# Five sums of squares per tile in two single-pass products instead of one 32-bit product

## The reference

```
x = layernorm(x + delta_rule_attention(x))     # ln1, and a norm over each head inside
x = layernorm(x + top-2-of-8 experts(x))       # ln2
x = layernorm(x + gated_linear_scan(x))        # ln3
x = layernorm(x + gated FFN of 3 stages(x))    # ln4

layernorm(x) = (x - mean(x)) / sqrt(var(x) + 1e-5)
inside the attention, for each head:
o = o * rsqrt(mean(o * o) + 1e-5) * norm_w
```

## Time and profile before

| | |
|---|---|
| median of 3 runs | 814.32 us (811.01 to 815.33) |
| the profiled execution | 817.33 us, of which the span shown is 815.3 us |
| PE busy | 752.2 us, 92% of the span |
| VectorE, ScalarE, GpSimd busy | 576.4, 499.7, 489.4 us |
| mean granted TensorE clock | 0.967 |
| the chain that ended last | PE 66%, DVE 11%, POOL 10%, ACT 5% |

### The profile page before, as it was taken

How to read it: one execution, slowest core, us unless ns; L and a number is a source line. 1 busy time by engine, 2 the same in 40 slices (tenths; PEclk the granted TensorE clock), 3 DMA queues, 4 the chain that set the end, 5 groups by cost and what they waited for, 6 DMA issues and landing times.

```text
span 815.3 us, 11346 instructions
## 1 busy us (share of the span) xinstructions
PE 752.2 (92%) x3492; PEld 579.7 (71%) x3492; DVE 576.4 (71%) x1146; ACT 499.7 (61%) x799; POOL 489.4 (60%) x503
## 2 busy tenths in 40 slices
PE   4999689888959999999989999999999999999996
PEld 3778567576547777767777778777876786777775
DVE  4677866779569757786768678867777777776553
ACT  3778444554755585468536855675577457767763
POOL 0049768579957766787675356534754475286353
PEclk9999896989979999999989999999999999999999
DMA  4025340652322320132012301400130120021000
GB/s 142 14 86 177 88 143 15 193 156 67 90 55 76 97 60 28 41 75 66 28 39 85 84 27 45 110 27 27 55 99 26 31 60 26 1 78 40 1 14 13
DMA packets 47244, 52.68 MB, mean 65 GB/s; under 512 B 2720, under 2 KB 31904, under 8 KB 47200
## 3 DMA queue, kind: packets, MB, share of 16 engines
q1 hardware_dynamic: 47200, 52.13, 22.0%
HBM read 38.62 MB, written 13.50 MB: 64 GB/s over the span
## 4 chain that ended last, share of the span: by engine, by line
PE 66%; DVE 11%; POOL 10%; ACT 5%; issue 5%; DMA 3%; SPq 0%; DVEq 0%; ACTq 0%; POOLq 0%
PE bank L461 66%; POOL fbl L1330 3%; POOL acc L1338 3%; POOL tmp L1270 1%; POOL tpm L1273 1%; DVE m L1632 1%; DMA pack<-pk 1%; POOL texp L1297 1%; DMA xs<-in_xh 1%; DVE sexp L1585 1%; DVE x L1568 1%; DVE spread L1577 1%; DVE yg L1595 1%; DVE x3h L1790 1%; DVE pk L1423 1%
## 5 line engine op out<-in xcount | busy, mean ns | idle before, releaser
L1330 POOL TENSOR_TENSOR fbl<-hf,fbh 128x512 fp32r<-128x512 f32 x64 | 90.0, 1406 | 44.1 <-ACT fbh L1127 43.5
L1270 POOL TENSOR_TENSOR tmp<-apm,tpm 128x31 f32<-128x31 f32 (+15 forms) x124 | 74.7, 603 | 55.4 <-DVE apm L1455 41.8
L1115 ACT ACTIVATE hf<-bank 128x512 f32<-128x512 f32 x64 | 38.3, 598 | 112.8 <-PE bank L461 97.7
L1773 DVE TENSOR_TENSOR fbl<-hf,fbh 128x512 fp32r<-128x512 f32 x64 | 68.9, 1077 | 48.4 <-ACT fbh L1121 48.4
L1273 POOL TENSOR_TENSOR tpm<-tpm,tmp 128x31 f32<-128x31 f32 (+15 forms) x124 | 76.6, 617 | 9.7
L1369 POOL TENSOR_TENSOR fbl<-hf,fbh 128x512 fp32r<-128x512 f32 x28 | 37.0, 1324 | 72.5 <-DVE fbh L1826 72.5
L1338 POOL TENSOR_TENSOR acc<-acc,yg 128x512 f32<-128x512 f32 x48 | 67.8, 1413 | 17.9 <-DVE yg L1595 17.9
L461 PE MATMUL bank<-fal,wfh 128*128 128x512 f32 x160 | 67.8, 424 | 0.0
L461 PE MATMUL bank<-fbl,wmh 128*128 128x512 f32 x128 | 58.8, 459 | 7.1 <-POOL fbl L1330 4.0
L461 PE MATMUL bank<-fah,wfh 128*128 128x512 f32 x160 | 62.5, 391 | 0.0
L461 PE MATMUL bank<-fah,wfl 128*128 128x512 f32 x160 | 62.3, 390 | 0.0
(11 more groups left out here) (238 smaller groups left out, 2146.3 us busy)
## 6 DMA issues: line engine op xcount, KB each, us to landing
gb<-gt SPq DMA_DIRECT2D x64, 256.0 KB, 3.2
pk<-pack SPq DMA_DIRECT2D x7, 1280.0 KB, 7.4
pack<-pk SPq DMA_DIRECT2D x5, 1280.0 KB, 7.1
ws<-in_wf SPq DMA_DIRECT2D x11, 256.0 KB, 3.6
pack<-pk SPq DMA_DIRECT2D x4, 640.0 KB, 4.4
xs<-in_xh SPq DMA_DIRECT2D x8, 262.0 KB, 2.8
xt<-in_xh SPq DMA_DIRECT2D x8, 262.0 KB, 3.0
ws<-in_wm SPq DMA_DIRECT2D x8, 256.0 KB, 3.7
```

What stands on the lines that cost most here:

```text
L1115: A.activation(hf[:, 0, :], bank[4][:, :], ACT.Gelu).then_inc(S["gelu_done"], 1)
L1270: G.tensor_tensor(m, a, r, ALU.mult).then_inc(S["t_mul"], 1)
L1330: G.tensor_tensor(fbl[:, sl, :], hf[:, 1, :], f32(fbh[:, sh, :]), ALU.subtract)\
L1773: tt(fbl[:, sl, :], hf[:, 0, :], f32(fbh[:, sh, :]), ALU.subtract).then_inc(S["lo0"], 1)
```

## The change

For 39 of the sums (eight each of the head sums and of ln1, ln2 and ln3, seven of ln4), ScalarE squares the tile twice: first with the output rounded to `F32R` (tiles `a5r`, `m4r`), then in full (`a2`, `m2`, `f2`), as before. VectorE subtracts the rounded squares from the full ones (`square_low`, `head_low`) into another rounded tile, the rest, which lies over the full squares (`a2r`, `m2r`, `f2r`). TensorE multiplies both, one single-pass product each, by a rounded copy of the constant matrix (`mean_r`, `head_r`), and adds them in the bank. It waits for the rounded squares before the first and for the rest before the second. Two copies at the program's start make `mean_r` and `head_r`. No tile takes new memory but `mean_r`.

The order changes in three places of a tail. `head_sums` moves on TensorE from behind `glu(1)` to behind `glu(2)`, and `var_product("2")` from behind `glu(2)` to behind `glu(3)`. On VectorE the subtractions are put between other work.

```diff
@@ tensor
             def var_product(n, t, src, bk):
-                pe.wait_ge(S["sq" + n], t + 1)
-                mm(bank[bk][:, :], mean_w, src[:, :]).then_inc(S["var" + n], 1)
+                pe.wait_ge(S["sq" + n], 2 * t + 1)
+                mm(bank[bk][:, :], mean_r[:, :], SQ_HIGH[n][:, :], stop=False)
+                pe.wait_ge(S[f"sq{n}_lo"], t + 1)
+                mm(bank[bk][:, :], mean_r[:, :], SQ_LOW[n][:, :], start=False).then_inc(S["var" + n], 1)
@@ head_sums
-                pe.wait_ge(S["osq_done"], a + 1)
+                pe.wait_ge(S["osq_done"], 2 * a + 1)
                 pe.wait_ge(*after("o_copied", CN * a + CN))
-                mm(bank[2][:, :], head_w, a2[:, :]).then_inc(S["oss_done"], 1)
+                mm(bank[2][:, :], head_r[:, :], a5r[:, :], stop=False)
+                pe.wait_ge(S["osq_lo"], a + 1)
+                mm(bank[2][:, :], head_r[:, :], a2r[:, :], start=False).then_inc(S["oss_done"], 1)
@@ tails on TensorE
                     glu(f, 1)
+                    glu(f, 2)
                 if a is not None:
                     head_sums(a)
                 if f is not None:
-                    glu(f, 2)
+                    glu(f, 3)
                 if m is not None:
                     var_product("2", m, m2, 1)
                 if f is not None:
-                    glu(f, 3)
                     pe.wait_ge(*after("g_act", FC * f + FC - 1))
@@ scalar (the same in head_squares and attention_square, with a5r)
                 act.wait_ge(*after("d" + n, t + 1))
+                A.activation(SQ_HIGH[n][:, :], src[:, :], ACT.Square).then_inc(S["sq" + n], 1)
                 A.activation(dst[:, :], src[:, :], ACT.Square).then_inc(S["sq" + n], 1)
@@ vector
+            def square_low(n, t, buf):
+                dve.wait_ge(S["sq" + n], 2 * t + 2)
+                tt(SQ_LOW[n][:, :], buf[:, :], f32(SQ_HIGH[n][:, :]), ALU.subtract).then_inc(S[f"sq{n}_lo"], 1)
+
+            def head_low(a):
+                dve.wait_ge(S["osq_done"], 2 * a + 2)
+                tt(a2r[:, :], a2[:, :], f32(a5r[:, :]), ALU.subtract).then_inc(S["osq_lo"], 1)
@@ ramp2 on VectorE (ramp3 alike)
+                head_low(a)
                 ...
                 unit_rows(s)
                 beta_rows(s)
+                square_low("1", a, a2)
                 attention_norm(a)
@@ dense on VectorE, behind gated(m, 3)
+                    if f is not None and e == 4:
+                        square_low("4", f, f2)
@@ tails on VectorE
                     glu(0)
+                    head_low(a)
                     glu(1)
+                    square_low("2", m, m2)
                     glu(2)
                     glu(3)
                 ...
-                    lru_input(m)
+                    lru_gx(m)
+                    square_low("1", a, a2)
+                    lru_m(m)
                 ...
                     attention_low(a)
+                    square_low("3", m, m2)
                     top_two(a)
@@ drain on VectorE, behind the cast of product 1
+                    if c == 1:
+                        square_low("4", l, f2)
```

More of the change, by code:

```diff
@@ L82, in build @@
         centre_w = sb("centre_w", [128, 128])
+        mean_r = sb("mean_r", [128, 128], F32R)
+        at_s3 = top[0]
         s3row = sb("s3row", [128, 128]); wsum = sb("wsum", [128, 24])
@@ L99, in build @@
         gb = sb("gb", [128, 2, W]); yg = sb("yg", [128, 2, W]); hf = sb("hf", [128, 2, W])
+        at_a = top[0]
         a1, a2, a3, a4, a5, oT = (sb(n, [128, W]) for n in ("a1", "a2", "a3", "a4", "a5", "oT"))
@@ L128, in build @@
         assert top[0] <= nc.sbuf_usable_end, top[0]
+        head_r = over("head_r", [128, 128], F32R, at_s3)
         wqkv = over("wqkv", [128, 3, 128], F32, temps)
@@ L196, in build @@
             texp_ready turn_done turn_ready in_done x_f x_ready os_done s_ready o_copied
+            osq_lo sq1_lo sq2_lo sq3_lo sq4_lo
             mixl_done mix_act mix_o o_ready osq_done oss_done ors_done og_done wo_done x1_hi
@@ L238, in f32 @@
             return ap.bitcast(F32)
+        a2r, a5r = (over(n, [128, W], F32R, at_a + 2048 * i) for n, i in (("a2r", 1), ("a5r", 4)))
+        m2r, m4r = (over(n, [128, W], F32R, temps + 2048 * i) for n, i in (("m2r", 1), ("m4r", 3)))
+        f2r = over("f2r", [128, W], F32R, at_f + 2048)
+        SQ_HIGH = {"1": a5r, "2": m4r, "3": m4r, "4": m4r}
+        SQ_LOW = {"1": a2r, "2": m2r, "3": m2r, "4": f2r}
         def by_seq(ap):
@@ L892, in drain @@
                     c = slice(g * W // 2, (g + 1) * W // 2)
-                    pe.wait_ge(S["sq4"], f + 1 + g)
+                    pe.wait_ge(S["sq4"], 2 * f + 1 + g)
                     mm(bank[3 - 3 * g][:, 0:W // 2], mean_w, f2[:, c]).then_inc(S["var4"], 1)
@@ L997, in head_squares @@
                 act.wait_ge(*after("o_ready", a + 1))
+                A.activation(a5r[:, :], a1[:, :], ACT.Square).then_inc(S["osq_done"], 1)
                 A.activation(a2[:, :], a1[:, :], ACT.Square).then_inc(S["osq_done"], 1)
@@ L1009, in attention_square @@
                 act.wait_ge(S["wo_done"], a + 1)
+                A.activation(a5r[:, :], bank[3][:, :], ACT.Square).then_inc(S["sq1"], 1)
                 A.activation(a2[:, :], bank[3][:, :], ACT.Square).then_inc(S["sq1"], 1)
@@ L1530, in _ @@
             tt(centre_w[:, :], ident, mean_w, ALU.subtract).then_inc(S["cen_ready"], 1)
+            V.tensor_copy(mean_r[:, :], mean_w)
             V.memset(sexp[:, :, :, :], 0.0)
@@ L1550, in _ @@
                     solve_out(0)
+                    V.tensor_copy(head_r[:, :], head_w)
                     V.memset(spread[:, 0:B, :, :], 0.0).then_inc(S["x_zero"], 1)
@@ L1837, in tails @@
                     glu(0)
+                if A_:
+                    head_low(a)
+                if F_:
                     glu(1)
+                if M_:
+                    square_low("2", m, m2)
+                if F_:
                     glu(2)
```

## The result

The changed kernel takes 823.47 us (median of 4 runs, 820.09 to 825.01) where the kernel before took 814.83 us beside it (4 runs, 811.01 to 817.67). The ratio is 1.0095, with a 95% interval of 1.0066 to 1.0124: it is slower, by 5 to 10 us. The forecast was 820.3 us.

What follows compares the result with a forecast made beforehand. TensorE was taken as the bound, tied with a second chain in every tail; 3.5 + 0 - 0.7 + 0 + 0.6 + 1.2 + 1.4 = 6.0 us on 814.32 gave 820.3 us, range 809 to 827.

Steps and rivals of the forecast that it cites:

- a second chain: Every tail: lru gates, tanh, ln1 square, table load, decay, scan, cast, GpSimd rest, hidden; claimed to tie with TensorE.
- step 4: Router at a steady tail's end: gate 1.8 later, TensorE 0.9 late; last GELU slips; next dense stage 0.7 late.
- TensorE's credit: TensorE saves 0.36 us a sum, 14.0 us over 39; rival that it arrives, in part or all, 0.14.
- Step 1: Steady tail, head and ln2 sums: credit 0.72, but the third gate product comes late; 0.2 us remains.
- Step 2: Steady tail, tied chain: extra ln1 square moves the table load +0.5; 0.2 earlier start leaves TensorE +0.3 us.
- Step 3: Steady tail, ln3's sum: the subtraction stands behind GpSimd's texp; TensorE is 0.5 us late.
- Dense stages: ln4 sums: wait for VectorE's bank about 0.6 instead of 0.20, no loss; two stages with triangular systems +0.3 each.
- signs named beforehand: Waits expected at gate product, GpSimd rest, gate_turn, yg and drain; table load 0.3 later; ln3 subtraction over 1.4 us.
- f = 5, f = 6, drain: Tail without t_spread: 0; tail without attention: -0.7; drain, ln4's sum waiting for its subtraction until 782.7: +1.2 us.
- The ramps: Second and third ramp: ln1's subtraction and extra squares delay chains, +0.7 us each, +1.4 together.
- the rival on the clock: Steady tails drop to 1.2 GHz: little chance; one more slow stretch gives 823; router or clock above 823: 0.16.

Runs made afterwards that it cites:

- e1: Changed kernel with only ln3's sum put back to one 32-bit product (no second square, no subtraction); 818.4 us.
- e3: Changed kernel with head sums and ln2's sum back to 32-bit products at their old place on TensorE; 822.3 us.
- e6: Changed kernel with the rest left out of all five sums: one rounded square, no subtraction, one single pass; 805.4 us.
- e8: Changed kernel with only ln4's sum put back to one 32-bit product; 820.0 us.
- e7: Changed kernel with two passes for head and ln3 alone, ln1, ln2, ln4 back, x1l behind the router's selection; 815.46 us, ratio 0.9986 to the kernel before.
- e2: Changed kernel with only ln1's sum put back to one 32-bit product; 822.6 us.
- e4: Changed kernel with ln3's subtraction moved ahead of x1l on VectorE; 827.6 us.
- e5: Changed kernel with ln3's subtraction ahead of the router's selection and x1l behind it; 822.4 us.
- e9: e7 with the router's gate weights moved right behind top_two, ahead of two casts and x1l; 816.75 us.
- e10: e5 with the same early gate weights, all five sums in two passes; 829.1 us.
- e11: e9 with the GELU table loaded ahead of the wait for GpSimd's rest and x1l behind the third cast; 814.63 us, ratio 0.998 to the kernel before.

## Why the prediction was right

The direction, its reason (TensorE ties with a second chain in every tail, and the change loads that chain) and the place (five tails, drain) held; e1 to e3, e6 and e8 show it part by part. That the size of a tail came out too is partly luck: steps 1 to 3 cost 0.78 where 0.5 was put down, and step 4, which was to lift that to 0.7 at the next stage, added nothing.

- **TensorE's credit.** 0.36 a sum was about right: 12.3 us less busy, and e7's tail of f = 5 shortens by 0.78 with two sums, 0.39 each.
- **Step 1**, forecast to keep 0.2, kept nothing. The third gate product was late and `hidden` began 0.27 earlier, as worked out. What I left out is the last chunk of `hidden`, which waits for GpSimd's last `fal` rest, 1.79 us long (608.54 in GpSimd's timeline). The first ln1 square moved by 0.03. e3 agrees: undoing this step leaves the period at 78.32.
- **Step 2**, forecast +0.3: +0.52, the second ln1 square in full, because step 1 had nothing to set against it. e2 gives back 0.45.
- **Step 3**, forecast +0.5 in all: the product behind the sum starts 0.78 late, of which 0.26 is this step's own, where I had 0.2. The wait (0.37) and the length (1.77) are those foreseen.
- **Step 4** failed. It had TensorE wait for `gate`, 0.9 late there and 0.7 in the next stage. The gate slipped by 1.72 (forecast 1.8), but TensorE, 0.28 later than forecast behind ln3's sum, came just with it: the products behind the sum are 0.78 late, `gate_turn` is 0.75 late, and no wait is marked between them. The last GELU, second in the step, lost the 0.90 of idle time that ScalarE had ahead of it, and no more: it still starts 0.03 behind TensorE's last product. So three chains now end the tail together, TensorE's own, the gate's and ScalarE's, and the first alone accounts for the 0.75. e1, which frees the other two and gives back 0.20, shows it. The tie is what e4, e5, e7, e9 and e10 each ran into. Of the signs named beforehand the wait for `gate` at `gate_turn` is the one that didn't come; the others did, the late table load with 0.52 in the place of 0.3.
- **Dense stages.** 0.60 of waiting in the place of 0.20, and nothing lost in the steady ones, as forecast. Between tails 0 and 1 it was +0.37 where 0.3 was put down. The +0.44 of the last dense stage I did not foresee: I had given a cost only to stages with triangular systems, and this one has none. e8 ties both to ln4. The stage between tails 1 and 2, also put at 0.3, costs about 0.9 at one clock (estimate above).
- **f = 5, f = 6, drain.** +0.2, -0.8 and +1.2 against 0, -0.7 and +1.2. The drain begins 1.15 us later in this trace. ScalarE's, VectorE's and TensorE's rows of it:

```profile
781.31 0.63 ACT L996 ACTIVATE m4r<-f 128x512 fp32r<-128x512 f32 x1 [2.08 <-DVE f L1946]
781.85 0.62 ACT L997 ACTIVATE f<-f 128x512 f32<-128x512 f32 x1
```

```profile
782.30 0.95 DVE L1941 CAST fah<-hf 128x512 fp32r<-128x512 f32 x1
783.17 0.68 DVE L1629 TENSOR_TENSOR f2r<-f,m4r 128x512 fp32r<-128x512 f32 x1
```

```profile
781.99 0.50 PE L472 MATMUL bank<-m4r,mean_r 128*128 128x512 f32 x1
783.90 0.50 PE L472 MATMUL bank<-f2r,mean_r 128*128 128x512 f32 x1 [1.41 <-DVE f2r L1629]
```

  The subtraction ends at 783.85 - 1.15 = 782.70, the very time put down, but on another way: it is held by the gate product and the cast ahead of it on VectorE, and meets no rest itself (0.68). Against the earlier trace rows, where TensorE ran on from 780.84 without a gap, it now waits 1.41 inside the sum.
- **The ramps**, +1.4, can't be judged: that stretch moves by 4 us between the profiled executions.
- **The clock.** The steady tails kept their 1.00, as the rival on the clock had it. But a stretch at a lower clock stood in the trace before and not in the one after, worth about 3.5 us, and it hides part of the loss when the two spans are compared.

The stages that can be compared as they stand sum to 3.9 + 0.2 - 0.8 + 0.4 + 0.4 + 1.2 = 5.3 us, against 3.5 - 0.7 + 0.3 + 1.2 = 4.3 forecast for them. With the estimate of 0.9 for the dense stage between tails 1 and 2 it is 6.2, near the 6.0 by which the runs differ at one granted clock. The medians differ by 8.6 with an interval of 5 to 10. The ramps are not in this account, and whether the change has a share there stays open.

## What to carry to other kernels

Work saved on the busiest engine counts only where no other chain arrives at the same time: align the two traces at a stage's first product and ask of each later mark how late the second comer is, before counting a credit. If a row names what was waited for, test it by moving it away; here the named gate hid a GELU that arrived with it, and a distance that stays the same in every variant (in the loop's tails 0.42 to 0.46 us from the GELU's end) pointed to it. Then ask what released that one too: in the changed kernel it was TensorE's own last product, in e7 a GpSimd rest. And read the granted clock of a stage before you read its length. A subtraction of two SBUF operands should be priced with what GpSimd does at that moment, in both directions.

## What the runs showed of the hardware

- A 128x4 TENSOR_SCALAR takes 1.26 and 1.22 us on VectorE while GpSimd runs two 128x512 subtractions (e7) and 0.16 and 0.17 with GpSimd idle (e9). The Trainium skill, page "SBUF — State Buffer", section "Who interferes with whom", counts `tensor_scalar` among the VectorE instructions that can take the port pair shared with GpSimd, and has the later of the two wait for the whole instruction. These rows agree, and a VectorE operand of four columns doesn't soften it.
- The hold works both ways: `texp`'s pair grew from 2.98 to 3.43 us, and the `fal` rests of e9 from 2.66 to 3.09, when a VectorE subtraction of two SBUF operands stood between the two GpSimd instructions.
- A load of ScalarE's table stands behind the wait of the instruction that needs it: 1.28 us came after a wait of 0.92 in e9, and before it in e11, where it was asked for ahead.
- TensorE's granted clock differed between executions in stretches of the same work: 0.92 and 1.00 in the dense stage between tails 1 and 2 (before, after), 0.88 and 1.00 in the drain (e2, after). The drain's stretch cost 1.65 us.
- The second of two ScalarE squares starts 0.48 to 0.54 us behind the first, although one lasts 0.59 to 0.63 on record.
